# Local layers: new orders of transfers, Gelus and products, and the row maxima subtracted on DVE instead of POOL

## The chip, the cores and the metric

The kernel runs on one core of a Trainium2 chip. The metric is the time of one execution on the device in microseconds (us), the median of several runs. The engines are called as in the profile: PE (TensorE, matrix products and transposes), DVE (VectorE), ACT (ScalarE), POOL (GpSimd), SP (SyncE, which here only issues transfers). Each engine works through its own queue in order; between engines only semaphores order the work.

## The reference, cut to what matters

The whole program is four residual stages over 16 sequences of 256 rows and 128 columns. The change touches only the third stage's second part, six pairs of a local-attention layer and a gated feed-forward layer, one after the other:

```python
for i in range(6):
    x = attn_layer(shift_tokens(x), Wqkv[i], q_scale[i], k_scale[i], Wo[i]) + x
    x = ffn_layer(shift_tokens(x), ln_g[i], ln_b[i], W1[i], b1[i], W2[i], b2[i]) + x

def attn_layer(x, ...):         # 16 heads of 64, windows of 32 rows
    q, k, v = split(x @ Wqkv)
    q, k = l2norm(q) * qs, l2norm(k) * ksc
    q = q * cos * scale + rotate_half(q) * sin * scale      # k likewise, with 1 / scale
    sim = einsum(q, [window before, own window] of k) * 8, masked
    out = softmax(sim) @ [the same windows of v]
    return out @ Wo

def ffn_layer(x, ...):          # 341 hidden columns
    xn = (x - mu) / sqrt(var + 1e-5) * g + bln
    a, gate = split(xn @ W1 + b1)
    return a * gelu(gate) @ W2 + b2
```

`shift_tokens` takes the second half of the columns from the row before. The softmax subtracts each row's maximum before the exponential; it is this subtraction that changes its engine.

## The kernel before

`local_layers` (line 778) runs 96 iterations `g`, one for each sequence in each of the six layers (`NB` = 16, `LAST` = 95), as a software pipeline. An iteration has two halves, `o=0` and `o=1`, one for each eight heads; `h = 2g + o` numbers the halves. In half `h` the kernel projects and rotates the queries and keys of half `h+2`, transposes those of `h+1`, and does scores, softmax and weighting of `h`. Beside it runs the feed-forward layer: in `o=0` the up products (`ups`, `hide_rows`), the attention's output product (`output`, `add_output`) and the transposed normed rows; in `o=1` the down product (`give`, `add_ffn`), the statistics of the next rows (`row_stats`, `deviations`) and the gate products (`gates`, `open_gates`).

Every engine has its order written out by hand in a function `iteration`. Those of the kernel before, for one half:

- **PE**: `project_rows` a=0 (L1085); in `o=0` `ups` (L1167, L1170), in `o=1` `give` (L1193); `scores` (L1114); `project_rows` a=1; `project_v` (L1091); in `o=0` `output` (L1154), in `o=1` `turn_x` (L1076) and `gates`, three gate products (L1167 twice, L1170 for the third); `turn_probs` (L1126); `turn_qk` (L1100); in `o=0` `turn_normed` (L1162); `weigh` (L1141).
- **DVE**: at the head of an iteration `normalise_rows` (L1437). In each half: `rotate` a=0 (L1387, L1391, twice each), `sum_squares` a=0 (L1396), `shift_scores` for both buffers e (mask L1406, maximum L1410); in `o=0` `hide_rows` (L1448), in `o=1` `add_ffn` (L1461, L1465) and `row_stats` (L1424, L1425, L1429); `invert_sums` for both buffers (L1415, L1417); `rotate` and `sum_squares` a=1; in `o=0` `add_output` (L1457).
- **POOL**: `add_sin` a=0 (L999, twice); `subtract_best` (L1030, twice); `weight` (L1036, twice); in `o=1` `deviations` (L1040, L1042); `add_sin` a=1; `norm`: fourteen small instructions (L1007 to L1015, the norm factors by Newton steps) and four products (L1023).
- **ACT**: `square` (L1268), `exps` (L1286), `move_v` (L1274), in `o=1` `move_x` (L1260, L1261), `move_probs` (L1291), `move_qk` (L1280), in `o=0` `move_normed` (L1303), in `o=1` `open_gates` (three Gelus, L1309 and L1313), `move_heads` (L1296). The two `warm` instructions (L1332 before the exponentials, L1356 before the Gelus) call for the table of the function that follows.
- **SP**: `stage_x` (L883), `send_v` of half 0 (store L900, then, once `heads_filled` says that the weighting has read the old v, four loads L908), `shift` of the rows for the next statistics (L888, L889, after `added`), `send_v` of half 1.

What the softmax of a half passes through: scores (PE), mask and maximum (DVE), subtraction (POOL), exponential (ACT), sum and inverse (DVE), product with the inverse (POOL), transposes (PE), copies (ACT), weighting (PE). The waits that order PE's gate products read:

```python
pe.wait_ge(f_freed, 3 * g + 3)          # L1176
pe.wait_ge(ffn_added, g + NB + 1)
hide(0)
```

The bank that holds the third gate or up product and the down product (`g_p`) also holds `out_p`, so `output` waits until `hide_rows` has read it (`g_freed`). `along(column, 64)` repeats a column over 64 elements as an operand.

## Time and profile before

| | us |
|---|---|
| median of 3 runs (lowest to highest) | 7089.07 (7083.05 to 7091.99) |
| the profiled execution | 7083.36 |
| its span | 7081.7 |
| busy in the span: PE, DVE, ACT, POOL | 5986.2, 4597.1, 3976.9, 3492.0 |
| local layers, about | 2230 to 6090 |

The span runs from the first to the last instruction; the profiled execution's own time is 1.7 us longer. A busy time is the sum of the durations of an engine's instructions. In the timeline rows below, the first number is the start in us from the span's start, the second the duration; "x4" stands for four instructions in a row merged into one line, and a bracket gives the time the engine sat idle before the line and the instruction whose end released it. Instructions of one engine overlap by some 0.08 us at their ends, so that the spacing of starts is a little shorter than a duration.

### The profile page before, as it was taken

The page shows a single profiled execution, that of the slowest core. Times are in us where ns is not written, and L with a number is a line of the kernel's source. Part 1 is how long each engine was busy: PE and PEld are TensorE (multiplying, and loading weights), DVE is VectorE, ACT ScalarE, POOL GpSimd, SP SyncE. Part 2 cuts the span into 40 slices and gives each one's busy share as a digit, 9 for nine tenths or more (in the row PEclk, how much of TensorE's full clock was granted, in tenths as well). Part 3 has the DMA queues.
Part 4 walks back from the last instruction along what each step waited for, and adds up shares of the span by engine and source line. Part 5 has one row for each costly group of instructions (what it writes and reads, how often), then busy time and mean ns, then how long its engine had stood idle before and what let it go on. Part 6 is the DMA issues. An engine that isn't in the chain of part 4 may idle for free. (4 is left out here: it accounts for less than half of the span.)

```text
span 7081.7 us, 219010 instructions
## 1 busy us (share of the span) xinstructions
PE 5986.2 (85%) x78552; PEld 4283.9 (60%) x78552; DVE 4597.1 (65%) x12075; ACT 3976.9 (56%) x9742; POOL 3492.0 (49%) x5407
## 2 busy tenths in 40 slices
PE   6999968889987888888888888888888888789998
PEld 4666656666655555555655655555555555567676
DVE  4555445555656777667666666766767667568378
ACT  4777547774234555555555555555555555446365
POOL 0000010000006888888888888888888888530020
PEclk9999979999999999999999999999999999879999
DMA  1000000000012333333333333333333333110210
GB/s 34 27 26 26 32 21 29 29 29 19 10 40 71 102 82 78 100 81 83 82 97 82 82 81 100 79 85 79 100 82 79 101 81 82 46 40 16 86 35 25
DMA packets 297443, 435.36 MB, mean 61 GB/s; under 512 B 56750, under 2 KB 139966, under 8 KB 296318
## 3 DMA queue, kind: packets, MB, share of 16 engines
q1 hardware_dynamic: 280958, 405.64, 21.7%
q0 software_dynamic: 7936, 24.28, 1.1%
q10 hardware_dynamic: 8448, 4.20, 0.2%
q8 instruction: 51, 0.84, 0.0%
q14 instruction: 50, 0.41, 0.0%
HBM read 256.81 MB, written 111.28 MB: 52 GB/s over the span
## 5 line engine op out<-in xcount | busy, mean ns | idle before, releaser
L1387 DVE TENSOR_TENSOR l_rot<-bank,l_cos 128x512 f32<-128x512 f32 x768 | 523.5, 682 | 870.7 <-ACT l_squares L1268 870.3
L999 POOL TENSOR_TENSOR l_rot<-l_rot,l_by_sin 128x512 f32<-128x512 f32 x768 | 966.6, 1281 | 92.7 <-DVE l_by_sin L1391 79.4
L1085 PE MATMUL bank<-w_w,l_x 128*128 (+1 forms) x1536 | 766.4, 621 | 71.6 <-issue 56.5
L1268 ACT ACTIVATE l_squares<-bank 128x512 f32<-128x512 f32 x768 | 458.7, 597 | 654.2 <-PE bank L1085 637.1
L1023 POOL TENSOR_TENSOR l_rot<-l_rot,l_norms 128x512 f32<-128x512 f32 x768 | 776.7, 1042 | 44.6 <-POOL l_norms L1015 44.4
L402 POOL DMA_DIRECT2D a_w<-in_a x23 | 13.0, 563 | 1482.6 <-PE bank L514 1359.4
L1036 POOL TENSOR_TENSOR l_probs<-l_probs,l_inverse 128x512 f32<-128x512 f32 x384 | 392.6, 1043 | 350.2 <-DVE l_inverse L1417 350.2
L1100 PE MATMUL bank<-ident,l_rot 128*128 128x128 f32 x3072 | 481.4, 290 | 91.6 <-ACT l_probs_t L1291 48.5
L1391 DVE TENSOR_TENSOR l_by_sin<-bank,l_sin 128x512 f32<-128x512 f32 x768 | 523.1, 681 | 5.8 <-POOL l_rot L999 5.8
L601 ACT ACTIVATE a_probs<-bank,a_neg_max 128x256 f32<-128x256 f32 x780 | 363.1, 476 | 271.3 <-DVE a_neg_max L712 271.3
L1280 ACT ACTIVATE l_qk<-bank 128x512 f32<-128x512 f32 x768 | 445.5, 596 | 112.8 <-PE bank L1100 109.0
L494 PE MATMUL bank<-ident,a_probs 128*128 128x128 f32 x2352 | 373.2, 281 | 149.4 <-DVE a_probs L722 149.4
L1291 ACT ACTIVATE l_probs_t<-bank 128x512 f32<-128x512 f32 x384 | 219.7, 597 | 493.4 <-PE bank L1126 493.4
L1154 PE MATMUL bank<-w_w,l_heads_t 128*128 (+1 forms) x3104 | 375.5, 280 | 141.0 <-DVE l_hidden L1448 140.7
L1154 PEld LDWEIGHTS bank<-w_w,l_heads_t 128*128 128x128 f32 x3104 | 357.5, 193 | 220.0 <-issue 220.0
L1396 DVE TENSOR_REDUCE l_square_sums<-l_squares 128x8 f32<-128x512 f32 x768 | 487.4, 677 | 0.0
L1100 PEld LDWEIGHTS bank<-ident,l_rot 128*128 128x128 f32 x3072 | 343.1, 146 | 217.2 <-issue 117.2
L1085 PEld LDWEIGHTS bank<-w_w,l_x 128*128 128x128 f32 x1536 | 261.5, 190 | 305.3 <-issue 297.9
L589 ACT ACTIVATE a_probs_t<-bank 128x512 f32<-128x512 f32 (+1 forms) x656 | 363.1, 565 | 123.8 <-PE bank L494 123.8
L712 DVE TENSOR_REDUCE a_neg_max<-bank 128x1 f32<-128x256 f32 x780 | 282.9, 418 | 226.8 <-PE bank L486 218.8
L486 PE MATMUL bank<-a_qk 64*128 64x256 f32 (+2 forms) x2660 | 423.6, 382 | 4.4 <-DVE a_qk L664 3.5
L1030 POOL TENSOR_TENSOR l_probs<-l_probs,l_best 128x512 f32<-128x512 f32 x384 | 410.0, 1088 | 20.0 <-DVE l_best L1410 19.7
(267 smaller groups left out, 14367.8 us busy)
## 6 DMA issues: line engine op xcount, KB each, us to landing
l_v<-l_values SPq DMA_DIRECT2D x768, 256.0 KB
l_values<-l_v_rows SPq DMA_DIRECT2D x192, 512.0 KB, 2.8
a_x<-normed_t SPq DMA_DIRECT2D x320, 128.0 KB, 2.0
l_stage_rows<-inner SPq DMA_DIRECT2D x98, 128.0 KB, 4.5
w_w<-in_w SPq DMA_DIRECT2D x6, 2048.0 KB, 10.2
l_shifted_half<-inner SPq DMA_DIRECT2D x98, 63.5 KB
f_w<-in_f SPq DMA_DIRECT2D x9, 514.5 KB
a_w<-in_a POOLq DMA_DIRECT2D x18, 256.0 KB, 2.9
```

The source lines that it names most:

```text
L486: last = nc.tensor.matmul(bank[:, t * SEQ + k0:t * SEQ + k1], queries, qk[p % 2][rows_of_head, keys_at + k0:keys_at + k1], start=True, sto ...
L999: nc.gpsimd.tensor_tensor(rot[s][n][:], rot[s][n][:], by_sin[n % 2][:], ALU.add).then_inc(summed, 1)
L1023: nc.gpsimd.tensor_tensor(mine, mine, along(norms[s][:, 8 * n:8 * n + 8], HD), ALU.mult)\
L1030: nc.gpsimd.tensor_tensor(mine, mine, along(best[:, e, :], HD), ALU.subtract).then_inc(shifted, 1)
L1085: nc.tensor.matmul(rows_p[i][:], x[:, tile_of(i)], layer_w(layer, quad * QUAD, QUAD), start=True, stop=True).then_inc(rows_filled, 1)
L1100: last = nc.tensor.transpose(t_p[i][:, tile_of(n)], rot[s][2 * a + i][:, tile_of(n)], core.ident[:])
L1154: last = nc.tensor.matmul(out_p[:, tile_of(i)], heads_t[:, pair, tile_of(i)], layer_w(layer, wo_at + pair * P, P), start=pair == 0, stop=p ...
L1268: nc.scalar.activation(squares[i][:], rows_p[i][:], ACT.Square).then_inc(squared, 1)
L1280: nc.scalar.activation(qk[o][:, :, 2 * a:2 * a + 2, W + i * P:W + (i + 1) * P], t_p[i][:].rearrange("p (n h s) -> p n h s", n=2, h=2), ACT ...
L1387: nc.vector.tensor_tensor(rot[s][2 * a + i][:], rows_p[i][:], cos[:, i, :], ALU.mult)
L1391: nc.vector.tensor_tensor(dst, src[:, :, ::-1, :], table, ALU.mult).then_inc(sin_done, 1)
L1396: nc.vector.tensor_reduce(square_sums[s][:, 8 * n:8 * n + 8], squares[i][:].rearrange("p (h d) -> p h d", d=HD), AX, ALU.add)\
```

## The change

On POOL, `subtract_best` goes; on DVE, each unit of `shift_scores` ends with the subtraction of its maxima, which waits for `max_ready`. DVE's order becomes: `rotate` a=0, `shift_scores`, in `o=0` `hide_rows`, then `sum_squares` a=0, `invert_sums`, and in `o=1` only then `add_ffn` and `row_stats`. `normalise_rows` uses another instruction.

On PE, `scores` and `project_rows` a=1 stand ahead of `ups`; `give` moves behind `turn_x`, just ahead of `gates`; the third gate product and its wait for `ffn_added` become `third_gate`, behind `turn_probs`. On ACT, `open_gates` moves from the end of `o=1` to the head of the next iteration, ahead of the exponentials; the squares of a=1 move behind the exponentials, and in `o=1` both exponentials come ahead of `move_x`. On SP, the loads of v become `fetch_v`, and that of half 0 is issued behind `shift` instead of ahead of it.

```diff
@@ counts
-            return 4 * g + 2 if not isinstance(g, int) or g <= LAST else 4 * LAST + 2 + 3 * (g - LAST)
-
-        def gates_fill(g):
-            return f_fill(g) + (4 if not isinstance(g, int) or g < LAST else 3)
+            return 4 * g + 3 if not isinstance(g, int) or g <= LAST else 4 * LAST + 3 + 3 * (g - LAST)
...
@@ SP, iteration and send_v
                     shift((g + NB - 1) & (NB - 1))
+                    if not last:
+                        fetch_v(g, 0)
...
                     if not last:
                         send_v(g, 1)
+                        fetch_v(g, 1)
...
                     store_v(h + 2, o, t_fill(h))
+
+                def fetch_v(g, o):
+                    h = 2 * g + o
                     sp.wait_ge(heads_filled, 4 * h + 4)
                     sp.sem_inc(begun, 1)
                     load_v(h + 2, o)
@@ POOL, iteration
                         if not last:
                             add_sin(h + 2, o, 0)
-                        subtract_best(h)
                         weight(h)
@@ PE
                     last.then_inc(f_filled, 1)
+
+                def hide_third(at):
                     nc.tensor.matmul(g_p, fw[:, at + 2 * P:at + 3 * P], normed_t[:], start=True, stop=True).then_inc(g_filled, 1)
...
                     pe.wait_ge(f_freed, 3 * g + 3)
+                    hide(0)
+
+                def third_gate(g):
                     pe.wait_ge(ffn_added, g + NB + 1)
-                    hide(0)
+                    hide_third(0)
...
                             project_rows(h + 2, o, 0, (g + 1) >> 4)
-                        if o == 0:
-                            ups(g)
-                        else:
-                            give(g)
                         scores(h, o)
                         if not last:
                             project_rows(h + 2, o, 1, (g + 1) >> 4)
+                        if o == 0:
+                            ups(g)
+                        if not last:
                             project_v(o, fill, (g + 1) >> 4)
                         if o == 0:
                             output(g)
                         else:
                             if not last:
                                 turn_x(g + 2, 3 * g + 3)
+                            give(g)
                             gates(g)
                         turn_probs(h, turned)
+                        if o == 1:
+                            third_gate(g)
@@ ACT, iteration
+                    open_gates(g)
                     nc.scalar.activation(warm[:], core.ones[:, 0:1], ACT.Exp)
...
+                        if o == 1 and not last:
+                            square(h + 2, 0, 0)
+                            square(h + 2, 0, 1)
+                        exps(h, 0)
+                        if not last:
+                            move_v(h + 2, 0, fill)
+                        exps(h, 1)
                         if not last:
                             if o == 1:
-                                square(h + 2, 0)
-                            square(h + 2, 1)
...
                                 move_x(g + 2, f_fill(g) + 2)
-                            exps(h, 1)
-                            nc.scalar.activation(warm[:], core.ones[:, 0:1], ACT.Gelu)
+                            square(h + 2, 1, 0)
+                            move_v(h + 2, 1, fill)
+                            square(h + 2, 1, 1)
                         move_probs(turned)
...
-                        else:
-                            open_gates(g)
                         move_heads(h, o)
@@ DVE
                     nc.vector.tensor_reduce(best[:, e, :], by_head(probs[e]), AX, ALU.max).then_inc(max_ready, 1)
+                    dve.wait_ge(max_ready, unit)
+                    nc.vector.tensor_tensor(by_head(probs[e]), by_head(probs[e]), along(best[:, e, :], HD), ALU.subtract)\
+                        .then_inc(shifted, 1)
...
-                            last = nc.vector.tensor_scalar(normed_rows[:, i, half * (D // 2):(half + 1) * (D // 2)], rows,
-                                                           mean_var[:, i, 0:1], rstd[:, i:i + 1], ALU.subtract, ALU.mult)
+                            last = nc.vector.scalar_tensor_tensor(normed_rows[:, i, half * (D // 2):(half + 1) * (D // 2)], rows,
+                                                                  mean_var[:, i, 0:1], rstd[:, i:i + 1].to_broadcast([P, D // 2]),
+                                                                  ALU.subtract, ALU.mult)
...
                             rotate(h + 2, o, 0)
-                            sum_squares(h + 2, o, 0)
                         shift_scores(h, 0)
                         shift_scores(h, 1)
                         if o == 0:
                             hide_rows(g)
-                        else:
+                        if not last:
+                            sum_squares(h + 2, o, 0)
+                        invert_sums(h, 0)
+                        invert_sums(h, 1)
+                        if o == 1:
                             add_ffn(g)
                             row_stats(g + 1)
-                        invert_sums(h, 0)
-                        invert_sums(h, 1)
```

The rest of the diff keeps the counts of semaphores and the first and last iterations in step with these orders.

## Rows read from the trace of the kernel before

**Rows 1.** Busy time by window: us, then busy us (count) by engine, clock, DMA
```profile
2230.00:6090.00 3860.00, 3196.69 (x60526) 2270.02 (x60526) 2695.98 (x5267) 2206.61 (x3945) 3221.64 (x5072) 0.98 0.34 86
```

**Rows 2.** Instructions of line 1176: durations in ns, first and last start
```profile
L1176 PEldq EVENT_SEMAPHORE  x95: 4528/4811/5345, 2226.8 to 6090.9; - x95
```

**Rows 3.** Waits of the local layers: total us, times, longest
```profile
POOL l_probs L1036 <- DVE l_inverse L1417: 343.8, 188, 4.0
```

**Rows 4.** Timeline of one iteration, PE
```profile
3903.73 1.98 PE L1085 MATMUL bank<-w_w,l_x 128*128 x4
...
3917.99 0.65 PE L1126 MATMUL bank<-ident,l_probs 128*128 128x128 f32 x4 [2.07 <-POOL l_probs L1036]
...
3924.97 1.98 PE L1085 MATMUL bank<-w_w,l_x 128*128 x4 [0.59 <-issue]
...
3934.80 3.83 PE L1154 MATMUL bank<-w_w,l_heads_t 128*128 x32 [1.44 <-DVE l_hidden L1448]
...
3938.47 1.04 PE L1126 MATMUL bank<-ident,l_probs 128*128 128x128 f32 x8
...
3944.53 1.99 PE L1085 MATMUL bank<-w_w,l_x 128*128 x4
```

**Rows 5.** Timeline of the same iteration, DVE in half o=1
```profile
3905.60 0.69 DVE L1387 TENSOR_TENSOR l_rot<-bank,l_cos 128x512 f32<-128x512 f32 x1 [5.10 <-ACT l_squares L1268]
...
3908.00 1.27 DVE L1396 TENSOR_REDUCE l_square_sums<-l_squares 128x8 f32<-128x512 f32 x2
...
3909.19 0.68 DVE L1406 TENSOR_TENSOR l_probs<-bank,masks 128x512 f32<-128x512 f32 x1
...
3909.90 0.69 DVE L1410 TENSOR_REDUCE l_best<-l_probs 128x8 f32<-128x512 f32 x1
...
3914.91 0.23 DVE L1424 BATCH_NORM_STATS2 l_stats<-l_shifted_half 128x6 f32<-128x64 f32 x1 [1.32 <-DMA l_shifted_half<-inner]
...
3915.87 0.63 DVE L1415 TENSOR_REDUCE l_sums<-l_probs 128x8 f32<-128x512 f32 x1
```

**Rows 6.** Timeline, DVE in half o=0
```profile
3926.84 0.69 DVE L1387 TENSOR_TENSOR l_rot<-bank,l_cos 128x512 f32<-128x512 f32 x1 [3.82 <-ACT l_squares L1268]
...
3933.06 1.26 DVE L1448 SCALAR_TENSOR_TENSOR l_hidden<-bank,w_f,l_gate 128x256 f32<-128x256 f32 x3
```

**Rows 7.** Timeline of the same iteration, POOL
```profile
3911.81 2.23 POOL L1030 TENSOR_TENSOR l_probs<-l_probs,l_best 128x512 f32<-128x512 f32 x2
...
3916.82 2.04 POOL L1036 TENSOR_TENSOR l_probs<-l_probs,l_inverse 128x512 f32<-128x512 f32 x2 [2.78 <-DVE l_inverse L1417]
...
3927.32 4.05 POOL L1023 TENSOR_TENSOR l_rot<-l_rot,l_norms 128x512 f32<-128x512 f32 x4 [0.24 <-POOL l_norms L1015]
...
3931.32 2.50 POOL L999 TENSOR_TENSOR l_rot<-l_rot,l_by_sin 128x512 f32<-128x512 f32 x2
```

**Rows 8.** DVE operations with two SBUF operands: min/median/max ns by line, and one
```profile
L1461 DVE TENSOR_TENSOR inner<-inner,w_f x99: 414/1300/1360, 2228.6 to 6175.6; 128x256 f32 x90, 128x256 f32<-128x256 f32 x9
...
3911.82 1.31 DVE L1461 TENSOR_TENSOR inner<-inner,w_f 128x256 f32 x1
...
L1470 DVE TENSOR_TENSOR l_cos<-rotary,l_scales x6: 1148/1217/1218, 2165.1 to 5443.7; 128x1024 f32<-128x1024 f32 x6
L1470 DVE TENSOR_TENSOR l_sin<-rotary,l_scales x6: 1199/2296/2300, 2166.2 to 5444.8; 128x1024 f32<-128x1024 f32 x6
```

**Rows 9.** Timeline: SP's shift, third gate, ACT's copies, Gelus, table load
```profile
3907.30 5.02 SPq L889 DMA_DIRECT2D l_shifted_half<-inner  x1
...
3915.33 0.59 PE L1170 MATMUL bank<-l_normed_t,w_f 128*128 128x256 f32 x2
...
3921.01 1.09 ACT L1280 ACTIVATE l_qk<-bank 128x512 f32<-128x512 f32 x2 [0.32 <-PE bank L1100]
...
3922.91 0.83 ACT L1309 ACTIVATE l_gate<-bank,w_f 128x256 f32<-128x256 f32 x2
...
3927.60 1.28 ACT L1332 ACT_TABLE_LOAD   x1
```

## What is predicted, and why

> **What bounds the kernel now.** I first read busy time by window, to find the stage the change touches. The local layers run from about 2230 to 6090 us, and no engine is full there: POOL is busy 3222 of 3860 us (83%), PE 3197 (83%), DVE 2696 (70%), ACT 2207 (57%) [rows 1]. So busy time alone does not name the limit, and a stage of 95 repeated iterations is limited by a loop of waits. The wait on the mark at the head of the gate product gives the period: 95 records from 2226.8 to 6090.9 us, so 3864.1/94 = 41.1 us [rows 2]. What is saved in one iteration counts 95 times.
>
> Next, the waits: POOL, the busiest, waits 343.8 us in 188 pieces, almost all of its idle time, for `inverse` before it weights the probabilities [rows 3]. Then one iteration, in order of time. I cut it where PE starts the first projection of a half: T1 = 3903.73 (half o=1), T0 = 3924.97 (half o=0), next T1 = 3944.53 [rows 4]. The halves take 21.24 and 19.56 us, 40.80 together. Each half has a mark of its own: the start of `turn_probs`, at T1+14.26 (3917.99) and T0+13.50 (3938.47). From it to the next cut go 6.98 and 6.06 us, PE's transposes alternating with ACT's copies, which the change hardly touches.
>
> Half o=1: DVE starts rotating at T1+1.87, has the maxima of both buffers by about T1+8.1 (3911.82), but starts `sums` only at T1+12.14 (3915.87), since `add_ffn` and `row_stats` stand ahead in its queue and `row_stats` waits 1.32 us for the shifted rows [rows 5]. POOL starts weighting 0.95 us after `sums` starts, and PE turns the first buffer 1.17 us after that (3916.82, 3917.99) [rows 4, 7].
> Half o=0: after the maxima DVE does `hide_rows` at T0+8.09 (3933.06) [rows 6]; PE's output product waits for that 1.44 us, starts at 3934.80 and holds PE until `turn_probs` at 3938.47 [rows 4]. Here DVE, then PE's output product, carry the time. POOL is close behind: its subtraction waits behind two sums with sines that end about 3933.8 [rows 7].
>
> **Part 1: inverse ahead of add_ffn and row_stats, half o=1.** New sum, from T1: 1.87 to the first rotation; 2.40 for four products (3905.60 to 3908.00); two units of mask, maximum, subtraction; then `sum_squares` 1.19 (3908.00 to 3909.19) [rows 5]. A unit is 0.71 (mask to the maximum that depends on it, 3909.19 to 3909.90), 0.71 by the same row for the new dependent subtraction, and 0.60 for the step after it (a 128x512 product, 2.40/4): 2.02, two are 4.04. `sums` then starts at 9.50, weighting at +0.95, turning at +1.17: 11.62 plus c1, the time DVE's subtractions wait (part 3). Against 14.26 this gains 2.64 - c1. The scores are no bound: without `give` ahead of them PE ends them near T1+3.5 (1.98 of projection, some 1.5 of their own), before DVE is free at T1+4.27.
> It pays two things. The third gate product now stands between `turn_probs` and `turn_qk`: its two instructions take 0.59 us [rows 9]. ACT's second copy of that stretch already waits 0.32 us for PE [rows 9], so I charge 0.38 (bounds: 0.59, all of it, and 0, if the alternation absorbs it). And `add_ffn`, which reads two SBUF operands, falls beside POOL's two weightings; where it fell beside POOL's pair of subtractions the pair took 2.23 instead of about 2.05, so 0.18 [rows 7]. Half o=1: 2.64 - 0.56 - c1 = 2.08 - c1.
> The wait for the shifted rows leaves the path. The shift moves ahead of the loads of v on SP's queue: it is issued behind `add_output`, near T0+16.5, instead of behind four loads at T1+2.7. From the start of its long part to the first statistic went 7.61 us (3907.30 to 3914.91) [rows 5, 9], so it lands by about T0+25, and DVE asks at T1+12 = T0+32. Cover: 7 us. Queued behind the shift are now the loads of v, some 2 us later; `weigh` wants them almost an iteration later. At worst that cover fails and the old 1.32 us returns.
>
> **Part 2: half o=0.** `hide_rows` starts after 1.87 + 2.40 + 4.04 = 8.31 + c0, against 8.09: each of the two units grows by 0.71, and the `sum_squares` that moved behind gives back 1.19. Loss 0.22 + c0; the 0.48 us to the output product and its 3.67 us are unchanged. POOL's weighting ends, by 8.31 + 1.18 (`hide_rows`) + 1.19 + 0.95 + 2.04 = 13.67 + c0, just ahead of the second turning at 14.2 + c0. The scores ahead of the ups save nothing here, for the masks wait for DVE.
> The Gelus move to the head of this half: two table loads of 1.28 us, three Gelus of some 0.43 us, between ACT's squares (done T0+2.62, where the table load starts now) and the first exponential: 2.62 + 1.28 + 1.3 + 1.28 + 0.2 = T0+6.7 [rows 9]. The subtraction delivers at 6.35 + c0, and `sums` reads only at 10.68 + c0: hidden, by 3 us. The last Gelu ends near T0+5.2, when PE, past scores and projections, comes to `ups` at 5.3: hidden, but without slack; 1 us of delay is still covered by `hide_rows` at 8.3. The `scalar_tensor_tensor` of the norm lies where DVE idled 3.82 and 5.10 us before its rotation: nothing, and neither gain nor loss from it on the path.
>
> **Part 3: the price of subtracting on DVE.** POOL loses four instructions of 1.02 us (4.1 us per iteration), but it is no longer what ends last, so none of that counts by itself. The subtraction reads two SBUF operands on DVE. The nearest operation is `add_ffn`'s first addition: unblocked 414 ns, median 1300 ns over 99. In the iteration shown it started with a POOL subtraction and took 1.31, that is 0.90 too long; `sin` of the tables, 2296 against 1217 for its twin, waited 1.08 behind a POOL sum [rows 8]. So DVE waits until the POOL operation in progress is nearly over (0.91 of a 1.01 us product, about 1.05 of a 1.25 us sum), then goes first, and POOL's next is late by some 0.45 us (0.18 for 256 elements, plus 256 more). Bounds for each subtraction: 0, and 1.08.
> The Trainium skill, "SBUF — State Buffer", section "Who interferes with whom", says that an operation of DVE with two SBUF inputs and one of GpSimd that reads SBUF block one another fully, the later one until the first finishes. The rows show a little less than the whole operation; what the rule's letter would give is rival (d).
> Where POOL stands: in half o=0 its weighting ends at T0+13.67+c0. From the end of weighting (3918.86) to the norm products (3927.32) went 8.46 us, 0.96 of it `deviations`, absent here: the products start at T0+21.17+c0. T1 is T0+19.78+c0, so they fill T1+1.39 to 5.41 (4.05 us [rows 7]) and two sums follow to 7.9. The first subtraction comes at 1.87+2.40+1.42 = 5.69, in the first sum, and waits until 6.46: 0.77. The second, at 8.48, finds POOL idle. c1 = 0.8 (0.5 to 1.0 if POOL is 0.3 us off).
> In half o=1, `deviations` waits for the later `row_stats`, and the next sums for rotations behind it. By the same rows the products start at T1+22.0+c1, while T0 comes at 11.62+0.56+6.98 = T1+19.16+c1: they start at T0+2.84, in steps of 1.01. The first subtraction (5.69) waits 0.09 for the third, the fourth is pushed by 0.45, the sum after it runs 7.34 to 8.59, and the second subtraction (7.80) waits until 8.39: 0.59. c0 = 0.68; with POOL 0.3 us later 0.96; with it 0.25 earlier both wait for a fresh operation, 1.68. I take 0.8.
>
> **Sum.** 2.08 - 0.22 - 0.8 - 0.8 = 0.26 us per iteration, 95 times: 25 us less. The profiled execution took 7083.4 us (span 7081.7), the median of the runs is 7089.1, 5.7 us above it. So 7058 for a profiled execution, 7064 for the median. With c0 0.68 to 0.96 and c1 0.5 to 1.0, and the third gate at 0 or 0.59, an iteration gains -0.31 to 1.06 us: 6988 to 7118 for the median, the likeliest case's own range.
>
> **Rivals.** (a) POOL stands badly in both halves. Mechanism: in half o=0 both subtractions meet an operation that has just started (0.84 each, c0 = 1.68) and in o=1 c1 is 1.0. Then 1.86 - 2.68 = -0.82 us: 78 us slower, 7167. It decides from c0 + c1 = 1.86, only 0.26 above my value; the phase needed, 0.25 us, is within what hand sums of 20 us can miss. Against it: the phases I get lie on the other side.
> (b) The subtractions hardly wait (c0 + c1 under 0.4, because POOL, relieved, has gaps there): 1.46 to 1.86 us an iteration, 139 to 177 us, 6912 to 6950. Against it the 1300 ns median in row after row.
> (c) Half o=1 gains less, since something else is late: the gate products wait for `x`, now moved after both exponentials. By the sum PE ends them at T1+11.1+c1, 0.5 us before the turning. If these, the third gate's wait for `add_ffn`, or the tight `ups` add 0.3 us, the change does nothing: 7089.
> (d) Each wait lasts for the whole POOL operation, 1.01 and 1.25 us (4.05/4, 2.50/2) [rows 7] instead of 0.91 and 1.05: 0.1 and twice 0.2 more, 0.26 - 0.5 = -0.24 us, 23 us slower, 7112. This is the letter of the skill's rule above. Against it speak the two measured waits of rows 8.
>
> **How the numbers follow.** Forecast 0.43, (a) 0.28, (b) 0.10, (c) 0.14, (d) 0.05. About 0.2% (14 us) can be told from no change. Forecast: 0.36 faster, 0.07 same; (a) 0.26 slower, 0.02 same; (b) faster; (c) 0.09 same, 0.05 slower; (d) slower. Together faster 0.46, same 0.18, slower 0.36. The range takes in (a) and most of (b): 6950 to 7180.
>
> **What would show it.** Right: `sums` of o=1 near T1+10.3 instead of 12.1, no wait of the statistics for the shifted rows, half o=1 shorter by 1 to 1.5 us, half o=0 longer by about 1 us; DVE's subtraction of 0.68 us showing means of 1.0 to 1.2 us by its waits. Wrong: subtractions near 0.68 (b), means above 1.4 (a), PE waiting for `x_moved` or `ups` for Gelus (c), or a half o=0 that got shorter, which would break the loop through `hide_rows`.

## The result, and the profile after

| | before | after |
|---|---|---|
| median of 3 runs, us | 7089.07 | 7165.72 (7161.59 to 7172.55) |
| ratio, 95% interval | | 1.0112 (1.0093 to 1.0132) |
| profiled execution, us | 7083.36 | 7161.59 |
| its span, us | 7081.7 | 7159.9 |
| mean granted TensorE clock | 0.964 | 0.949 |

The change makes the kernel 77 us slower. The forecast was 25 us faster; the time lies in the range, at the number of rival (a), but not by rival (a)'s mechanism. One execution of a later run, e3, took 22662 us at a granted clock of 0.60 and is left out of its ratio. The first view after the times is the busy time of each engine over the whole span, from the page of the kernel after (us, share, instructions):

```profile
PE 6135.5 (86%) x78558; PEld 4371.4 (61%) x78558; DVE 4829.1 (67%) x12459; ACT 3958.9 (55%) x9650; POOL 3190.7 (45%) x5023
```

POOL lost 301 us and DVE took on 232: the work went where the diff sends it. But PE, whose products only changed their order, is busy 149 us longer, which no term of the sum foresaw. One iteration shows where. The timeline of PE in the kernel after, the one that answers to [rows 4] (start, duration, line, in brackets the idle time before it and what ended it):

```profile
3900.23 1.98 PE L1080 MATMUL bank<-w_w,l_x 128*128 x4
...
3912.34 0.65 PE L1121 MATMUL bank<-ident,l_probs 128*128 128x128 f32 x4 [0.75 <-POOL l_probs L1032]
...
3919.55 1.98 PE L1080 MATMUL bank<-w_w,l_x 128*128 x4 [0.64 <-issue]
...
3930.62 5.46 PE L1149 MATMUL bank<-w_w,l_heads_t 128*128 x32 [2.46 <-DVE l_hidden L1458]
3935.92 1.04 PE L1121 MATMUL bank<-ident,l_probs 128*128 128x128 f32 x8
```

The next iteration begins at 3941.97. So half o=1 takes 3919.55 - 3900.23 = 19.32 us instead of 21.24 and half o=0 3941.97 - 3919.55 = 22.42 instead of 19.56: 41.74 us an iteration, 0.94 more than in [rows 4]. Times 95 that is 89 us. The mean over the loop is 41.14 us before and 41.94 after, 0.80 more, which is 76 us and agrees with the 77 measured. The row to look at is the output product, `output`: the same 32 products took 3.83 us in [rows 4] and take 5.46 here. Nothing interrupts them. The windows around that product in the kernel after (us; busy us and count of PE, PEld, DVE, ACT, POOL; granted clock; DMA share; GB/s):

```profile
3926.28:3928.16 1.88, 1.88 (x5) 0.57 (x3) 1.81 (x3) 1.23 (x2) 1.88 (x2) 1.00 0.00 0
3928.16:3930.62 2.46, 0.00 (x0) 0.01 (x1) 2.46 (x5) 0.63 (x1) 1.93 (x2) 1.00 0.00 0
3930.62:3933.00 2.38, 2.38 (x12) 2.38 (x13) 2.31 (x7) 1.57 (x3) 0.77 (x1) 0.58 0.06 22
3933.00:3935.92 2.92, 2.92 (x22) 2.92 (x21) 2.92 (x6) 0.00 (x0) 2.92 (x4) 0.76 0.43 161
```

PE works, then stands still for 2.46 us while DVE ends its second subtraction and does `hide_rows`; then it starts the product and the granted clock is 0.58 and 0.76, that is 1.2 GHz for much of it instead of 2.4. In the kernel before PE stood still for 1.44 us at this place ([rows 4]; the window below takes in 1.40 of it) and ran the product at full clock:

```profile
3933.40:3934.80 1.40, 0.00 (x0) 0.00 (x1) 0.92 (x3) 0.00 (x0) 1.40 (x3) 1.00 0.00 0
3934.80:3938.47 3.67, 3.67 (x32) 3.67 (x33) 2.79 (x6) 2.12 (x4) 2.97 (x4) 1.00 0.13 50
```

It is not one iteration. The groups of instructions of both kernels for this product, first before, then after (busy us, mean ns of one | idle time of PE ahead of them and what ended it):

```profile
L1154 PE MATMUL bank<-w_w,l_heads_t 128*128 x3008 | 360.3, 278 | 135.7 <-DVE l_hidden L1448 135.7
```

```profile
L1149 PE MATMUL bank<-w_w,l_heads_t 128*128 x2944 | 481.6, 340 | 228.9 <-DVE l_hidden L1458 228.9
```

Of the first 95 output products, those of the loop, 83 take over 4.3 us after the change and none before; the 83 exceed 3.83 us by 132 us in all. DVE's rows of the same iteration of the kernel after answer to [rows 5, 6]:

```profile
3902.10 0.69 DVE L1393 TENSOR_TENSOR l_rot<-bank,l_cos 128x512 f32<-128x512 f32 x1 [7.01 <-ACT l_squares L1275]
...
3905.93 1.09 DVE L1418 TENSOR_TENSOR l_probs<-l_probs,l_best 128x512 f32<-128x512 f32 x1
...
3908.38 0.69 DVE L1418 TENSOR_TENSOR l_probs<-l_probs,l_best 128x512 f32<-128x512 f32 x1
...
3910.18 0.68 DVE L1424 TENSOR_REDUCE l_sums<-l_probs 128x8 f32<-128x512 f32 x1
...
3925.26 1.02 DVE L1418 TENSOR_TENSOR l_probs<-l_probs,l_best 128x512 f32<-128x512 f32 x1
...
3927.63 1.32 DVE L1418 TENSOR_TENSOR l_probs<-l_probs,l_best 128x512 f32<-128x512 f32 x1
3928.88 1.25 DVE L1458 SCALAR_TENSOR_TENSOR l_hidden<-bank,w_f,l_gate 128x256 f32<-128x256 f32 x3
```

L1418 is the new subtraction. Its work is 0.69 us; what stands above that is its wait for a POOL operation: 0.40 and 0 in half o=1, 0.33 and 0.63 in half o=0. Over the stage:

```profile
L1418 DVE TENSOR_TENSOR l_probs<-l_probs,l_best x384: 691/1067/1562, 2204.3 to 6215.5; 128x512 f32<-128x512 f32 x192
```

The columns are the shortest, median and longest in ns, then the first and last start. The stage lasts 4011 us by this row; by the mask's row of the kernel before (first start 2204.6, last 6132.6) it lasted 3928, 83 less.

### The profile page after: what moved, and what is told of

The parts are those of the page before. It is cut to its first block and busy times, and to the rows that moved or that the text cites. A ratio compares the mean times of both kernels' runs of the same rounds, so it can differ in the third digit from the quotient of the medians.

```text
span 7159.9 us, 219024 instructions
## 1 busy us (share of the span) xinstructions
PE 6135.5 (86%) x78558; PEld 4371.4 (61%) x78558; DVE 4829.1 (67%) x12459; ACT 3958.9 (55%) x9650; POOL 3190.7 (45%) x5023
## 5 line engine op out<-in xcount | busy, mean ns | idle before, releaser
L1001 POOL TENSOR_TENSOR l_rot<-l_rot,l_by_sin 128x512 f32<-128x512 f32 x768 | 1006.8, 1333 | 95.0 <-DVE l_by_sin L1397 95.0
L1080 PE MATMUL bank<-w_w,l_x 128*128 (+1 forms) x1536 | 804.5, 631 | 74.0 <-issue 58.4
L1025 POOL TENSOR_TENSOR l_rot<-l_rot,l_norms 128x512 f32<-128x512 f32 x768 | 810.3, 1088 | 44.7 <-POOL l_norms L1017 44.2
L1032 POOL TENSOR_TENSOR l_probs<-l_probs,l_inverse 128x512 f32<-128x512 f32 x384 | 409.8, 1088 | 695.2 <-DVE l_inverse L1426 695.2
L1149 PE MATMUL bank<-w_w,l_heads_t 128*128 (+1 forms) x3104 | 507.3, 340 | 238.2 <-DVE l_hidden L1458 238.2
L1149 PEld LDWEIGHTS bank<-w_w,l_heads_t 128*128 128x128 f32 x3104 | 489.5, 252 | 317.1 <-issue 317.1
L1293 ACT ACTIVATE l_probs<-l_probs 128x512 f32<-128x512 f32 x384 | 241.9, 630 | 616.3 <-DVE l_probs L1418 611.5
L1080 PEld LDWEIGHTS bank<-w_w,l_x 128*128 128x128 f32 x1536 | 246.4, 190 | 362.5 <-issue 355.0
```

The costliest lines, as they stand in the source:

```text
L1001: nc.gpsimd.tensor_tensor(rot[s][n][:], rot[s][n][:], by_sin[n % 2][:], ALU.add).then_inc(summed, 1)
L1025: nc.gpsimd.tensor_tensor(mine, mine, along(norms[s][:, 8 * n:8 * n + 8], HD), ALU.mult)\
L1032: nc.gpsimd.tensor_tensor(mine, mine, along(inverse[:, e, :], HD), ALU.mult).then_inc(probs_ready, 1)
L1080: nc.tensor.matmul(rows_p[i][:], x[:, tile_of(i)], layer_w(layer, quad * QUAD, QUAD), start=True, stop=True).then_inc(rows_filled, 1)
L1149: last = nc.tensor.matmul(out_p[:, tile_of(i)], heads_t[:, pair, tile_of(i)], layer_w(layer, wo_at + pair * P, P), start=pair == 0, stop=p ...
```

## The experiments

Two theories. **The clock**: the waits of the subtractions are as small as forecast, and what makes the change slow is that the longer idle ahead of the output product makes TensorE's granted clock fall. **The waits alone**: the subtraction's contention with POOL is worth the whole loss, and the slow product brings the iteration to its end at the same time with or without its clock, since something else is late. Each run is compared with the kernel before run beside it (7083.64, 7085.76 and 7083.65 us on the three chips).

| run | median us | ratio to before (95%) |
|---|---|---|
| e1: after, idle filled by two products | 7067.39 | 0.9977 (0.9967 to 0.9986) |
| e10: after, filled by one | 7070.82 | 0.9984 (0.9974 to 0.9993) |
| e6: before, idle lengthened | 7389.06 | 1.0433 (1.0416 to 1.0450) |
| e2: after, `hide_rows` earlier | 7021.25 | 0.9912 (0.9896 to 0.9929) |
| e7: e2, idle filled | 7001.48 | 0.9884 (0.9868 to 0.9901) |
| e3: after, POOL subtracts | 7031.02 | 0.9923 (0.9907 to 0.9940) |
| e8: the kernel of e3 again, for its trace | 7033.41 | 0.9929 (0.9909 to 0.9949) |
| e4: before, DVE subtracts | 7444.15 | 1.0506 (1.0488 to 1.0523) |
| e5: e10, one operand from PSUM | 6880.87 | 0.9712 (0.9696 to 0.9728) |
| e9: after, mask added by PE | 6583.47 | 0.9296 (0.9280 to 0.9312) |

**Fill the idle: e1 and e10.** PE makes the second product of v again, twice more in e1 and once more in e10, in half o=0 only. The operands are there and the bank is its own, so no wait changes; PE has more work in the time in which it stood still.

```diff
-                def project_v(o, fill, layer):
+                def project_v(o, fill, layer, again=0):
...
+                        for _ in range(again * i):
+                            nc.tensor.matmul(t_p[i][:], x[:, tile_of(i)], layer_w(layer, wv_at + o * QUAD, QUAD), start=True,
+                                             stop=True)
...
-                            project_v(o, fill, (g + 1) >> 4)
+                            project_v(o, fill, (g + 1) >> 4, 2 if o == 0 else 0)
```

> The changed kernel, with the product for v's second tile made three times instead of once in half o=0 (the same values, so nothing else changes): PE is busy for 1.9 us more of the 2.46 us in which it otherwise stands idle ahead of the output product. Theory 1 (the idle stretch lowers TensorE's clock, granted 0.58 and 0.76 in the output product against 1.00 before it): the output product takes 3.7 to 3.9 us instead of 5.46, half o=0 gets 1.6 us shorter, and the time falls by 95 x 1.6 = 150 us, to 6995 to 7040. Rival (the output product is slow for what runs beside it, DVE and POOL on SBUF): it still takes 5.4 us and the time stays at 7166 within 15.

Timeline and window of the output product in e1:

```profile
3936.76 3.83 PE L1152 MATMUL bank<-w_w,l_heads_t 128*128 x32 [0.46 <-DVE l_hidden L1461]
```

```profile
3936.76:3940.43 3.67, 3.67 (x33) 3.67 (x34) 3.60 (x9) 1.57 (x3) 2.07 (x3) 1.00 0.38 143
```

With work added and nothing taken away the kernel gets faster, by 1.0112 - 0.9977 = 1.35% or 96 us. The product starts at the same word from DVE, after 0.46 us of idle instead of 2.46, at clock 1.00, and takes 3.83 us again. The waits are still there, and a little longer (mean of the subtraction 1115 ns, against 1054 in the kernel after). So the theory of the waits alone falls: with the waits kept and the clock held, the change is 0.23% faster than before, 16 us. The expectation's 150 us was too much: not every product was slow, so that only 132 us were to be had, and the longer waits take some 23 of them (61 ns, four times in 95 iterations). The trace's record of the clock gives an estimate of the same size: from the first to the 95th output product it is at its lower level for 379 us after the change, 157 before, 174 in e1. If PE is busy all that time, half of it is lost at half speed: (379 - 174)/2 = 102 us.

> The changed kernel with v's second tile made twice (once more) in half o=0, as a control for the run with one operand, which differs from it in that operand alone. Theory 1 (the clock decides in the output product and 0.9 us of work is enough to hold it): 7060 to 7080, as with two repetitions. Rival (a shorter fill leaves a gap of 1.5 us and the clock falls in part of the iterations): 7085 to 7140.

With one product 82 of the 95 output products are as fast as before, and 13 are not: all 12 behind 1.9 to 2.2 us of idle, 1 of 14 behind 1.6 to 1.9, and none behind less. The expected time came, and part of the rival with it. One of either kind, in the timeline of PE in e10:

```profile
3938.04 5.46 PE L1152 MATMUL bank<-w_w,l_heads_t 128*128 x32 [1.94 <-DVE l_hidden L1461]
...
3979.73 3.83 PE L1152 MATMUL bank<-w_w,l_heads_t 128*128 x32 [1.59 <-DVE l_hidden L1461]
```

**Lengthen it in the kernel before: e6.** One reduction by DVE ahead of `hide_rows`, 1.15 us, whose output nobody reads; it reads one SBUF operand and is no subtraction.

```diff
                         if o == 0:
+                            nc.vector.tensor_reduce(idle[:], cos[:].rearrange("p i (h d) -> p (i h) d", d=HD), AX, ALU.add)
                             hide_rows(g)
```

> The kernel before with one more operation on DVE ahead of hide_rows (a reduction of a table into a tile of its own, 1.1 to 1.2 us, one SBUF operand), and nothing else: PE's idle stretch ahead of the output product grows from 1.4 to about 2.6 us. Theory 1 (the length of that stretch decides whether TensorE's clock falls): the output product takes 5.4 instead of 3.83 us in most iterations, and an iteration costs 1.15 + 1.6 us: 7300 to 7350. Rival (the clock falls in the changed kernel for another reason, such as its new order of products): the output product stays at 3.83 and only the 1.15 us are added, 7170 to 7200.

Output product, its idle, its first stretch, and a stretch of half o=1 of the same iteration, all of e6:

```profile
3934.23 5.39 PE L1155 MATMUL bank<-w_w,l_heads_t 128*128 x32 [2.57 <-DVE l_hidden L1449]
```

```profile
3931.66:3934.23 2.57, 0.00 (x1) 0.01 (x1) 2.57 (x5) 1.92 (x4) 1.62 (x2) 0.98 0.00 0
3934.23:3936.00 1.77, 1.77 (x8) 1.77 (x9) 1.70 (x6) 0.20 (x1) 1.35 (x2) 0.50 0.32 120
3915.45:3919.00 3.55, 3.21 (x18) 2.61 (x19) 3.55 (x7) 1.86 (x4) 3.47 (x5) 0.72 0.00 0
```

The kernel before, with its subtraction on POOL, shows the same slow product as soon as the idle is about 2.57 us: 91 of 95. An instruction of 1.15 us, 109 us in 95 iterations, costs 303 us. That is more than was expected: the mechanism was right, but a second low stretch came in half o=1, from `turn_probs` into `turn_qk` (0.72 in the window above, behind 2.33 us of idle), which the expectation had left at full clock.

**Take the wait out of the loop instead: e2 and e7.** In e2 DVE does `hide_rows` between the two units of `shift_scores`. In e7 PE moreover transposes the identity eight times into the bank of the scores (already read) after `output` and after `give`.

```diff
                         shift_scores(h, 0)
-                        shift_scores(h, 1)
                         if o == 0:
                             hide_rows(g)
+                        shift_scores(h, 1)
```

```diff
+                def keep_busy(h, n):
+                    pe.wait_ge(masked, 2 * h + 2)
+                    for i in range(n):
+                        nc.tensor.transpose(s_p[0][:, tile_of(i % 4)], core.ident[:], core.ident[:])
...
                             output(g)
+                            keep_busy(h, 8)
...
                             give(g)
+                            keep_busy(h, 8)
```

> The changed kernel with hide_rows between the two units of shift_scores instead of behind both. Theory 1 (the loop of half o=0 runs through hide_rows and the output product, and the idle ahead of it costs the clock): hide_rows starts some 2.7 us earlier, PE goes from the projections to the output product without a long gap and at the full clock, turn_probs then waits for POOL's weighting at about T0+13.9 instead of T0+16.4; an iteration is 2.4 us shorter, 6920 to 6960. Rival (DVE's queue as a whole bounds the half): the weighting comes no earlier and the time stays within 30 us of 7166.

> The changed kernel with hide_rows between the units (as in the run before, 7021) and eight transposes of the identity into a bank that is free then, behind the output product in o=0 and behind give in o=1, where TensorE's clock still fell 28 and 34 times. Theory 1 (each low stretch costs about half its length in PE's work): the 239 us of low clock go to below 60, the time falls by 60 to 100 us, to 6920 to 6960. Rival (the low stretches there lie in slack, or the transposes delay the path): 7010 to 7040.

Timeline of e2, then the local layers of e2 and of e7 in one window each:

```profile
3913.95 3.81 PE L1149 MATMUL bank<-w_w,l_heads_t 128*128 x32
3919.45 0.65 PE L1121 MATMUL bank<-ident,l_probs 128*128 128x128 f32 x4 [1.69 <-POOL l_probs L1032]
```

```profile
2230.00:5990.00 3760.00, 3221.34 (x59834) 2247.50 (x59838) 2897.50 (x5589) 2160.62 (x3813) 2906.49 (x4648) 0.97 0.34 88
```

```profile
2230.00:5990.00 3760.00, 3333.68 (x61434) 2356.39 (x61434) 2934.30 (x5606) 2161.43 (x3822) 2913.77 (x4653) 0.99 0.34 88
```

In e2 nothing is idle ahead of the output product any more, and the kernel gains 142 us on the change (1.0112 - 0.9912), but 60 us less than the least expected: the idle moved behind the product, to `turn_probs`, which waits 1.69 us for POOL's weighting, and a part of the low clock moved with it. e7 brings the clock to 0.99 and yet gains only 0.28%, 20 us, over e2: its time at the lower clock fell from 215 to 68 us. That expectation failed: 7001 us lies above its range and just under that of its rival. Most of the stretches that went lay at `turn_probs` and `turn_qk`, where PE waits for POOL's weighting and ACT's copies. So low clock seems to cost only where PE carries the time; but this is argued, for e7 does not tell slack from a delay by the eight transposes themselves.

**Separate the two halves of the change: e3, e8 and e4.** e3 and e8 have all of the change but leave the subtraction on POOL. e4 is the kernel before with the subtraction on DVE and nothing else; its diff is the part of the change that takes `subtract_best` from POOL to DVE. The edit of e3 and e8:

```diff
...
+                        subtract_best(h)
                         weight(h)
...
-                    dve.wait_ge(max_ready, unit)
-                    nc.vector.tensor_tensor(by_head(probs[e]), by_head(probs[e]), along(best[:, e, :], HD), ALU.subtract)\
-                        .then_inc(shifted, 1)
```

> The changed kernel with all its new orders, but the subtraction of the maxima back on POOL. Theory 1 (the subtraction on DVE costs 0.71 us in each unit, the waits for POOL, 1.4 us per iteration, and through the gap the clock, 1.6 us): hide_rows starts near T0+6.9, no gap of over 1.5 us and the full clock, while POOL has to subtract behind its sums with sines again; 39.0 to 40.3 us an iteration, 6920 to 7040. Rival (the new orders themselves cost the time, by the third gate, the Gelus or give): slower than the kernel before, over 7089.

> The new orders with the subtraction on POOL once more, for its trace: 7029 as before. Its granted clock over the whole span was 0.954, less than the kernel before had. Theory 1: hide_rows starts near T0+6.9 and the output product runs at the full clock in most iterations, and the low stretches lie ahead of turn_probs, where PE now waits for POOL; rival: the output product itself takes 5.4 us here too.

> The kernel before with one part of the change alone: DVE subtracts the maxima, all orders are the old ones. Theory 1: half o=0 loses 1.4 us of dependent subtractions and about 1 us of waits ahead of hide_rows, and PE's gap ahead of the output product grows from 1.4 to over 3 us, so that the clock falls there too and costs 1.6 us more; half o=1 still waits for the shifted rows and loses little. 3.5 to 4.5 us an iteration, 7400 to 7520. Rival (no clock effect, POOL's relief pays for part): 7089 to 7300, and the output product at 3.8 us.

The two halves of one iteration of e8 and a stretch of the second; under them the row at which that stretch starts:

```profile
3908.62:3928.23 19.61, 18.00 (x332) 12.85 (x333) 13.08 (x24) 12.73 (x23) 17.15 (x29) 1.00 0.36 88
3928.23:3947.60 19.37, 16.11 (x269) 11.13 (x264) 14.95 (x32) 9.51 (x18) 15.78 (x22) 0.91 0.34 84
3940.11:3944.00 3.89, 3.89 (x15) 3.27 (x16) 3.61 (x11) 2.69 (x5) 2.05 (x4) 0.57 0.36 135
```

```profile
3940.11 1.53 PE L1169 MATMUL bank<-l_normed_t,w_f 128*128 128x256 f32 x4 [3.00 <-issue]
```

The new orders alone gain 0.77% (54 us), as e3 expected; moving the subtraction to DVE on top of them costs 1.0112 - 0.9923 = 1.89%, 134 us. In e8 half o=0 runs at full clock; half o=1 still pays for one low stretch, after 3.00 us of idle ahead of the gate products, for which the row names no releaser. By the program's order they wait for ACT's copies of `x`, moved behind both exponentials, and the second of these ends at 3940.01, 0.10 us before them. The expectation had put the stretch at `turn_probs`.

e4's output product and its window:

```profile
3921.56 6.40 PE L1147 MATMUL bank<-w_w,l_heads_t 128*128 x32 [3.88 <-DVE l_hidden L1444]
```

```profile
3921.56:3927.79 6.23, 6.23 (x32) 6.23 (x33) 4.60 (x10) 0.00 (x0) 5.40 (x8) 0.57 0.22 84
```

In the old order `sum_squares` still stands ahead of `hide_rows`, so the idle is 3.88 us in this iteration (3.54 in the mean), and 94 of 95 output products are slow, by 1.81 us in the mean. Without the new orders the move costs 361 us, as expected.

**What the second SBUF operand costs: e5.** Its control is e10. In place of the subtraction DVE adds the mask once more to the scores in PSUM: as many elements, one SBUF operand of full width fewer. The maxima are not subtracted.

```diff
                     dve.wait_ge(max_ready, unit)
-                    nc.vector.tensor_tensor(by_head(probs[e]), by_head(probs[e]), along(best[:, e, :], HD), ALU.subtract)\
-                        .then_inc(shifted, 1)
+                    nc.vector.tensor_tensor(probs[e][:].rearrange("p (n k) -> p n k", k=P),
+                                            s_p[e][:].rearrange("p (n k) -> p n k", k=P),
+                                            core.window_mask.unsqueeze(1).to_broadcast([P, 4, P]), ALU.add).then_inc(shifted, 1)
```

> The changed kernel with v's second tile made twice in half o=0 (to hold the clock), and in place of the subtraction DVE adds the mask to the scores from PSUM a second time: an operation of the same size that reads one SBUF operand instead of two. The maxima are then not subtracted, so this part of the softmax is left out. Theory 1 (the second SBUF operand makes DVE wait for POOL, 1.0 us in half o=0 and 0.4 us in half o=1): these operations take 0.68 us each instead of 1.06, and 95 x 1.4 = 135 us less than the filled kernel's 7067: 6920 to 6950. Rival (DVE's longer durations are hidden, or not from the operand): 7050 to 7075.

Groups of this line in e10 and, replaced, in e5:

```profile
L1421 DVE TENSOR_TENSOR l_probs<-l_probs,l_best 128x512 f32<-128x512 f32 x376 | 418.1, 1112 | 13.1
```

```profile
L1421 DVE TENSOR_TENSOR l_probs<-bank,masks 128x512 f32<-128x512 f32 x368 | 254.4, 691 | 12.8
```

The operation falls to 690 to 694 ns in all 384 rows of it, and the kernel to 0.9712 from 0.9984: 193 us, against 135 expected. (1112 - 691) ns, four times in 95 iterations, are 160 us. The rest is put down to the clock, which is at its lower level for 147 us of the loop in e10 and 55 in e5; half of that difference, 46 us, would be more than enough, and no run separates the two.

**A version that beats both: e9.** The same softmax, with the mask added by PE: a product of the identity with the mask, in bf16, closes the accumulation of the scores. DVE then takes both the maximum and the subtraction straight from PSUM.

```diff
-                                        start=True, stop=True)
...
+                                        start=pair == 0 and i == 0, stop=False)
+                    for e in range(2):
+                        nc.tensor.matmul(s_p[e][:].rearrange("p (n k) -> p n k", k=P), ident_half[:],
+                                         mask_half[:].unsqueeze(1).to_broadcast([P, 4, P]), start=False, stop=True)\
+                            .then_inc(scores_filled, 4)
...
-                    nc.vector.tensor_tensor(probs[e][:].rearrange("p (n k) -> p n k", k=P),
-                                            s_p[e][:].rearrange("p (n k) -> p n k", k=P),
-                                            core.window_mask.unsqueeze(1).to_broadcast([P, 4, P]), ALU.add).then_inc(masked, 1)
-                    dve.wait_ge(masked, unit)
-                    nc.vector.tensor_reduce(best[:, e, :], by_head(probs[e]), AX, ALU.max).then_inc(max_ready, 1)
+                    nc.vector.tensor_reduce(best[:, e, :], by_head(s_p[e]), AX, ALU.max).then_inc(max_ready, 1)
                     dve.wait_ge(max_ready, unit)
-                    nc.vector.tensor_tensor(by_head(probs[e]), by_head(probs[e]), along(best[:, e, :], HD), ALU.subtract)\
+                    nc.vector.tensor_tensor(by_head(probs[e]), by_head(s_p[e]), along(best[:, e, :], HD), ALU.subtract)\
```

> The changed kernel with the mask added by PE instead of DVE: a product of the identity with the mask (both copied to bfloat16, 512 columns, one for each buffer) closes the accumulation of the scores in PSUM; DVE takes the maximum from PSUM and subtracts it from PSUM into SBUF, so that the subtraction reads one SBUF operand and one operation of 0.6 to 0.7 us falls away in each unit. Theory 1 (the two dependent steps and the waits for POOL carry both halves): a unit takes 1.3 us instead of 2.0 and waits for nothing, PE's added products cost some 0.5 us a half, and an iteration gets 4 us shorter than in the changed kernel: 6700 to 6860. Rival (PE, with products added, or POOL bounds both halves by then): no shorter than with one operand and the mask on DVE, 6870 to 6960.

Of e9: the window of the local layers, the group of the subtraction, the mask's product and the output product in PE's timeline:

```profile
2230.00:5650.00 3420.00, 3207.47 (x61699) 2262.94 (x61698) 2555.95 (x5333) 2184.66 (x3897) 2871.34 (x4730) 1.00 0.38 98
```

```profile
L1417 DVE TENSOR_TENSOR l_probs<-bank,l_best 128x512 f32<-128x512 f32 x381 | 263.5, 692 | 13.2
```

```profile
3930.11 0.60 PE L1115 MATMUL bank<-l_mask_half,l_ident_half 128*128 128x512 bf16 x2
...
3935.45 3.83 PE L1152 MATMUL bank<-w_w,l_heads_t 128*128 x32
```

6583 us, 7% under the kernel before and 8% under the one after, and under the expectation's lower end. The period of the iteration shown falls from 41.74 to 35.82 us, by 5.92. Three terms are taken from rows: the four masks of 0.71 us on DVE's path [rows 5], 2.84; the four waits, 4 x (1054 - 692) ns = 1.45; the output product, 5.46 - 3.83 = 1.63. Together 5.92. The agreement to a hundredth is luck, since over the loop the mean falls by 6.08 (41.94 to 35.86), but no large term is missing. PE pays 0.60 us a half for it, within time that it spent waiting. In this kernel it goes into the output product without idle and is busy for 3207 of 3420 us, so that there a still shorter path on DVE would bring little.

## Why the prediction went wrong, point by point

**The failed step** stands in part 2: "the 0.48 us to the output product and its 3.67 us are unchanged". The 0.48 held (3928.88 + 1.25 to 3930.62 are 0.49); the 3.67 did not. The longer idle was in the sum: 1.44 us in [rows 4] plus a `hide_rows` later by 0.22 + 0.8 makes 2.46 us. That the row of after has just 2.46 is luck, for `hide_rows` came later than that and PE's projections ended later too. The prediction counted this idle as waiting that ends when DVE is done. It has a second price, the clock of what follows: from the product's start to `turn_probs` went 5.30 us instead of 3.67, 1.63 more, in the iteration shown. Over the loop the slow products make 132 us. The miss is 7165.72 - 7064 = 102; the other terms, below, came out better by 0.64 us in half o=1 and worse by 0.22 in half o=0, in the iteration shown, together 40 us better in 95 iterations, and 132 - 40 = 92.

The trace of before held a warning that the prediction did not read. Its loop has 157 us at the lower clock, in 31 stretches, all in half o=1 and all at the gate products, `turn_probs` or `turn_qk`. One is in the iteration after that of [rows 4]: the first two gate products take 2.07 us there, behind 2.24 us of idle, where those of after take 1.10 at full clock.

```profile
3955.48 2.07 PE L1167 MATMUL bank<-l_normed_t,w_f 128*128 128x256 f32 x4 [2.24 <-issue]
```

```profile
3955.30:3958.70 3.40, 2.92 (x6) 1.85 (x6) 2.76 (x11) 2.10 (x3) 1.08 (x2) 0.50 0.23 86
```

**Half o=0** lost 2.86 us where 1.02 was forecast. `hide_rows` starts at 3928.88 = T0+9.33, which is 8.31 + 1.02: c0 was 1.02, not 0.8, and 0.96 of it are the two waits in the rows. So 0.22 + 1.02 + 1.63 = 2.87. The first two terms were right to some 0.2 us.

**Half o=1** gained 1.92 us where 1.28 was forecast. `turn_probs` starts at T1+12.11; the sum gave 11.62 + 0.8. The waits were 0.40 us instead of 0.8 in the iteration shown. From there to T0 go 7.21 us: the third gate and `add_ffn` cost 0.23 over the 6.98 of before, not 0.56. `sums` starts at 3910.18 = T1+9.95, near the mark that the prediction gave.

**The waits**, 0.96 + 0.40 = 1.36 in the iteration shown and 4 x (1054 - 691) ns = 1.45 in the mean, lie between the forecast's 1.6 and rival (b). Rival (a) asked for 2.68, and its time came out by another mechanism: a right number is no proof of the reason. Rival (d) is out, too. In the kernel after 256 of the 384 subtractions take over 0.3 us more than 691 ns and started while a POOL operation of the same size was running; in every one of them the last 691 ns begin 0.14 us before that POOL operation ends by the trace (0.137 to 0.147). So the wait follows the POOL operation in progress and ends a little before it, as part 3 had it. Rival (c) did not come about in the iteration shown: the gate products end at T1+11.36, and PE then still waits 0.75 us for POOL's weighting. The Trainium skill, "SBUF — State Buffer", section "Who interferes with whom", states the full block between a DVE operation with two SBUF inputs and a GpSimd one that reads SBUF, and none for a DVE operation with at most one outside its two-port modes. Both parts agree in kind with the rows here: 1054 ns with two, 691 and 692 in e5 and e9 with one. Part 3 was right to give these waits a large term (some 160 us of e5's gain are theirs); what it did not see is that an operand from PSUM takes them away altogether.

**The covers** held. DVE's first statistic no longer waits for the shifted rows; its group in the kernel after has 0.1 us of idle time in all:

```profile
L1433 DVE BATCH_NORM_STATS2 l_stats<-l_shifted_half 128x6 f32<-128x64 f32 x186 | 39.8, 214 | 0.1
```

The Gelus did not delay `hide_rows`, which follows the second subtraction without a gap (3927.63, 3928.88). POOL, relieved of four operations, only waits more for `inverse`, 658.5 us where [rows 3] has 343.8, so that part 3 was right to count none of its 4.1 us:

```profile
POOL l_probs L1032 <- DVE l_inverse L1426: 658.5, 183, 5.9
```

**The sum as a whole.** With the clock held in most or all output products, by e10 and e1, the change is 13 to 16 us faster than before, where the forecast was 25. That is close partly by luck, since the terms of the two halves missed by 0.64 and 0.22 us in opposite directions and e1's waits are longer. The terms that were worked out were sound in kind; the one that was set to nothing decided.

## What to carry to other kernels

Count the idle time ahead of a long block of products twice: as the wait, and as the clock at which the block may then run; look in the trace for places where the granted clock already falls behind such idle, and ask whether the change lengthens the idle ahead of the block. Before work goes from POOL to DVE, count the SBUF operands of the operation: with one of them taken from PSUM it ran at 691 ns, with two at 1054 to 1115. Filling idle time with products that nobody needs paid 96 us in e1, where PE carries the time, and 20 us in e7, where it seems mostly to wait; shortening the wait itself paid more (142 us in e2, 193 in e5).

## What the runs showed of the hardware that was not expected

TensorE's granted clock fell inside a loop in which PE is busy 83% of the time before the change and 85% after it. Ahead of the 95 output products of the loop: 1.2 to 1.6 us of idle in 94 iterations of the kernel before and 66 of e10, and none of these products was slow; 1.9 to 2.2 us in 12 of e10 and 4 of the kernel after, and all were; 2.2 to 2.6 us in 82 iterations of the kernel after, and 71 were; the same in 86 of e6, and 83 were; over 2.6 us in 94 of e4, and all were. The level changes late in the idle or as PE starts again: in the kernel after the low stretch begins inside the product in 58 of the 83 cases and ahead of it in 25, in e6 ahead of it in 90 of 91. The product then starts at 0.50 to 0.58. The Trainium skill, "TensorE: Matmul & The Clock Gate", section "A second HAM failure mode: psum-queue depth-cycling", describes a kernel in which short idle times between groups of products make the clock swing between its two levels; the rows of after, e4 and e6 agree with that, and put its price at 1.5 to 1.8 us in the mean, 2.6 in the row of e4, for a product of 3.83. The length of the idle alone does not decide: 11 of those 82 products of the kernel after kept their clock, and in half o=1 of the kernel before PE idles for over 1.7 us at one place or another in every iteration ([rows 4] has 2.07) while the clock falls in 31 of 94. What else of PE's past decides, these runs do not settle.

A single-instruction cost can be multiplied: 1.15 us more of DVE in e6 cost 3.2 us an iteration (303/95), through two low stretches. And PE can take over a masking addition for 0.60 us a half, as one more product in the accumulation of the scores, where DVE took 1.42.
